# GpSimd issues its transfers by index in pairs and waits for each pair's landing

## Chip, core and metric

The kernel runs on one core of one Trainium2 chip. The core has five engines that run their own programs and meet at semaphores: TensorE (PE), VectorE (DVE), ScalarE (ACT), GpSimd (POOL) and SyncE (SP). The metric is the device time of one launch in microseconds, median of the timed runs.

## What is computed

A stack of residual layers over x of 32 x 256 tokens with 128 numbers each. The part that matters here is the feed-forward L0_ffn, which stands before and after an attention and sends each token to two of eight experts:

```python
def _L0_ffn_ref(x, gate_w, gate_b, w1, b1, w3, b3, w2, b2, sw1, sb1, sw3, sb3, sw2, sb2):
    xt = x.reshape(-1, D)
    logits = xt @ gate_w.T
    scores = jax.nn.softmax(logits.astype(jnp.float32), axis=-1)
    biased = scores + gate_b.astype(jnp.float32)
    idx = jax.lax.top_k(biased, TOP_K)[1]
    weights = (jnp.take_along_axis(scores, idx, axis=-1) * ROUTE_SCALE).astype(x.dtype)
    cw = jnp.sum(jax.nn.one_hot(idx, E, dtype=x.dtype) * weights[..., None], axis=1)
    h1 = jnp.einsum('td,efd->etf', xt, w1) + b1[:, None, :]
    h3 = jnp.einsum('td,efd->etf', xt, w3) + b3[:, None, :]
    a = swiglu(h1 * h3)
    y = jnp.einsum('etf,edf->etd', a, w2) + b2[:, None, :]
    routed = jnp.einsum('te,etd->td', cw, y)
    sh = swiglu((xt @ sw1.T + sb1) * (xt @ sw3.T + sb3))
    shared = sh @ sw2.T + sb2
    return (routed + shared).reshape(inp_shape)
...
x = x + 0.5 * _L0_ffn_ref(_layernorm(x, axis=-1), ...)
x = x + _L0_attn_ref(_layernorm(x, axis=-1), ...)
x = x + 0.5 * _L0_ffn_ref(_layernorm(x, axis=-1), ...)
x = x + 0.5 * _L1_ffn_ref(_layernorm(x, axis=-1), ...)
x = x + _L1_attn_ref(_layernorm(x, axis=-1), ...)
x = x + 0.5 * _L1_ffn_ref(_layernorm(x, axis=-1), ...)
```

## The kernel before

**Tiling.** The 8192 tokens are 16 chunks of 512; a chunk is 4 tiles of 128 tokens, one a partition. x stays in the on-chip memory for the whole run. The 16 chunks form three groups of 4, 6 and 6. The two passes of L0_ffn are l = 0 and l = 1; the attention lies at the start of the second pass.

**One pass for a group.** A "head" step normalises a chunk, makes the gate's logits and the shared expert's part, and leaves the rows in fp16 halves in `rows` (a view of `store`). The "route" steps on DVE choose two experts and compute for each token its place among its expert's rows, `r_slot`. POOL then *scatters*: for tile t and choice i one indirect DMA (L1914) writes 128 rows of 512 bytes from `rows` to the table `row_dram[g]` in HBM, at the places in `r_slot`. When all scatters of the group have landed, SP loads the table's rows back, transposed, into `u_xp` (L1979, `load_rows`, which waits for `scattered[g]`), PE, ACT and DVE run the experts on them in units of 512 rows, and ACT stores the results to the table `ys` in HBM. POOL *fetches*: for a chunk eight indirect DMAs (L1930), by choice and tile, each 128 rows of 512 bytes from `ys` to `y_in` at the places in `r_result`. There are two buffers `y_in`, for even and odd chunks. DVE waits for all eight (`fetched[c % 2]`), multiplies them by the weights and adds them to x (L1135, `weighed`). There are 128 x 2 = 256 scatters and 256 fetches.

**POOL's other work** are the small powers for the norms: `rstd_entry` (L1880), `rstd_head` (L1885), `gn_r_head` (L1895), `rstd_mid`, `rstd_front` and `rstd_last` (L1874, L1876). DVE or ACT wait for each of them.

**Order.** Each engine runs its steps in an order that is written out by hand, as a string of letters for each engine (`turns`); for POOL "s" is one scatter step (two DMAs), "f" one fetch, "a", "b" and "c" are the heads of three lanes. Two heads' work is interleaved with two lanes of units. `Waiting.wait_ge` leaves out a wait for a value that the engine has already waited for. Before the change POOL waits for no landing of its own DMAs: it goes on when a DMA's descriptors are made. A DMA adds 16 to its semaphore when it has landed.

Of the kernel before, what the change touches and what calls it, by code (L numbers as in the profile page):

```python
# [20 lines left out]
T = 4  # L21
# [119 lines left out]
def build(nc, dram, packed, x_in, out):  # L141
# [14 lines left out]
    with ExitStack() as ctx:  # L156
# [1711 lines left out]

        def pool_program(pool):
            on = Waiting(pool)  # L1870

            def root(s, which, c, a, b):
                on.wait_ge(*s.by_vector.at("mv", which, c))
# [32 lines left out]
            def scatter(l, g, t):  # L1906
                c = groups[g].first + t // T
                on.wait_ge(*route.by_vector.at("slot", l, c // 2))
                on.wait_ge(*heads[c % LANES].by_vector.at("rows", l, c))
                if l:  # L1910
                    for u in (groups[g].units - 2, groups[g].units - 1):
                        on.wait_ge(*unit_lanes[u % 2].by_tensor.at("h", l - 1, g, u, 0, 0))
                for i in range(2):
                    pool.indirect_dma_start(  # L1914
                        row_dram[g], bass.IndirectOffsetOnAxis(route.slot[g][:, i, t:t + 1].bitcast(U32), 0),
                        rows[:, groups[g].first * T + t, :, :].rearrange("p k d -> p (k d)"), None).then_inc(scattered[g], 16)

            def fetches(l, c, n):
                g, t0, i = group_of[c], (c - groups[group_of[c]].first) * T, c % 2
                k, t = divmod(n, T)  # L1920
                if n == 0:
                    for j in range(2):
                        last = load_index((l, g, groups[g].units - 1))
                        on.wait_ge(y_stored[(last + j) % 2], 16 * ((last + 1 + j) // 2))
                    on.wait_ge(*route.by_vector.at("result", l, g))
                    if l or c >= 2:
                        l2, c2 = divmod(l * chunks + c - 2, chunks)
                        reader = mids[c2 % 2] if l2 else heads[c2 % LANES]
                        on.wait_ge(*reader.by_vector.at("weighed", l2, c2, 1))
                pool.indirect_dma_start(  # L1930
                    fetch.y[i][:, t, k, :], None, y_dram[g],
                    bass.IndirectOffsetOnAxis(route.result[g][:, k, t0 + t:t0 + t + 1].bitcast(U32), 0)).then_inc(fetched[i], 16)
# [256 lines left out]
```

## Time and profile before

| | us |
|---|---|
| three timed runs: median (lowest to highest) | 1219.88 (1218.39 to 1219.9) |
| the profiled execution, first to last instruction | 1611.3 |
| of it busy: PE, DVE, ACT, POOL | 1208.2, 1037.9, 881.7, 645.2 |
| POOL in 256 scatters, in 256 fetches | 258.8, 262.2 |
| POOL waiting for its issue before scatters, before fetches | 70.8, 70.3 |

The profiled execution is a third longer than the timed ones. Its durations are read one by one, and its idle times with care: a timed run has less of them. A POOL row of a DMA is the time in which POOL makes its descriptors, not the time to its landing. "issue" is a gap that nothing visible released. Waits of an engine stand under the instruction that waited, with what released it.

### The profile page before, as it was taken

How to read it: one execution, taken by the hardware profiler on the slowest of the kernel's cores; microseconds unless marked ns; L12 is line 12 of the kernel's file. 1: busy time of each engine (PE TensorE's matmuls, PEld its weight loads, DVE VectorE, ACT ScalarE, POOL GpSimd, SP SyncE). 2: the span in 40 equal slices, each digit the busy share in tenths (PEclk: the TensorE clock that was granted, in tenths of full speed). 3: DMA queues.
4: the chain of work that ended last, by engine and by line, in shares of the span. 5: the costliest groups of instructions: out<-in, count | busy, mean ns of one | idle time of the engine just before them, and what ended most of it. 6: DMA issues, size and time to landing. Idle time of an engine off the chain costs nothing.

```text
span 1611.3 us, 37336 instructions
## 1 busy us (share of the span) xinstructions
PE 1208.2 (75%) x14084; PEld 950.7 (59%) x14113; DVE 1037.9 (64%) x3441; ACT 881.7 (55%) x1505; POOL 645.2 (40%) x679
## 2 busy tenths in 40 slices
PE   3745767567766778767666766799989897989997
PEld 2423545455555666555554645677877676768776
DVE  7954655455645656666664664677767757888774
ACT  3545556334544445645543653676677445766764
POOL 1364443344555455555545453431322323342100
PEclk9876878787887978988887887898898978999989
DMA  8012323223132322222132222311210101010001
GB/s 263 14 50 62 79 68 75 59 63 83 57 84 70 78 71 76 62 65 55 57 87 67 68 67 66 76 43 46 56 46 23 28 18 33 15 29 24 2 9 34
DMA packets 172875, 93.77 MB, mean 58 GB/s; under 512 B 98516, under 2 KB 163183, under 8 KB 172575
## 3 DMA queue, kind: packets, MB, share of 16 engines
q1 hardware_dynamic: 115886, 35.64, 9.0%
q0 software_dynamic: 16384, 33.59, 7.3%
q10 hardware_dynamic: 40432, 22.17, 4.9%
q8 instruction: 118, 1.93, 0.5%
q14 instruction: 55, 0.44, 0.1%
HBM read 25.78 MB, written 45.61 MB: 44 GB/s over the span
## 4 chain that ended last, share of the span: by engine, by line
PE 37%; DVE 22%; ACT 13%; another core or an unknown queue 13%; issue 12%; POOL 1%; DMA 1%; ACTq 0%; POOLq 0%; DVEq 0%; SPq 0%
PE bank L759 8%; PE bank L581 3%; PE bank L820 2%; PE bank L967 2%; PE bank L806 2%; PE bank L839 2%; DVE x L1135 2%; PE bank L775 2%; PE sums L984 1%; PE sums L901 1%; PE bank L532 1%; PE sums L904 1%; ACT heads_store L1674 1%; DVE heads_store L1189 1%
## 5 line engine op out<-in xcount | busy, mean ns | idle before, releaser
L1914 POOL DMA_INDIRECT rows<-store,r_slot x256 | 258.8, 1011 | 185.1 <-DVE r_slot L1396 114.1
L759 PE MATMUL bank<-u_xp,w_hi 128*128 128x128 f16 x2432 | 267.3, 237 | 83.7 <-issue 74.0
L1930 POOL DMA_INDIRECT y_in<-ys,r_result x256 | 262.2, 1024 | 120.6 <-issue 70.3
L759 PE MATMUL bank<-u_xp,w_lo 128*128 128x128 f16 x1216 | 245.7, 237 | 34.6 <-issue 34.4
L759 PEld LDWEIGHTS bank<-u_xp,w_hi 128*128 x2432 | 212.3, 108 | 100.0 <-issue 94.4
L759 PEld LDWEIGHTS bank<-u_xp,w_lo 128*128 x1216 | 130.3, 107 | 47.1 <-issue 47.1
L581 PE MATMUL bank<-heads_store,w_hi 128*128 128x512 f16 x256 | 92.6, 449 | 7.0 <-DVE r_lg L1164 4.2
L1874 POOL TENSOR_SCALAR ve_last<-mv_last 128x4 f32<-128x4 f32 x16 | 3.1, 195 | 215.0 <-DVE mv_last L1092 214.9
L1698 ACT ACTIVATE heads_store<-bank,sc 128x512 f32<-128x512 f32 x64 | 43.3, 682 | 75.0 <-PE bank L581 41.1
L1135 DVE SCALAR_TENSOR_TENSOR x<-y_in,r_weight,x 128x128 f32<-128x128 f32 x256 | 72.5, 346 | 1.1
L1189 DVE TENSOR_TENSOR heads_store<-bank,heads_store 128x512 f32<-128x512 f32 x64 | 43.7, 686 | 42.7 <-ACT heads_store L1698 33.9
L1885 POOL TENSOR_TENSOR rstd_head<-ve_head,half_neg 128x4 f32<-128x4 f32 x32 | 34.6, 1082 | 88.1 <-DVE ve_head L1097 86.8
L1481 DVE TENSOR_TENSOR u_gated_even<-bank,u_gated_even 128x512 f32<-128x512 f32 x38 | 26.0, 685 | 66.7 <-ACT u_gated_even L1769 34.6
L1665 ACT COPY heads_store<-bank 128x1024 f16<-128x1024 f16 x32 | 32.3, 1009 | 54.6 <-remote 32.3
L967 PE MATMUL bank<-store 32*64 32x64 f32 x2048 | 49.6, 239 | 15.6 <-issue 12.1
L1625 DVE TENSOR_TENSOR store<-store,bank 128x512 f32<-128x512 f32 x64 | 40.9, 681 | 25.0 <-PE bank L967 14.9
L581 PE MATMUL bank<-heads_store,w_lo 128*128 128x512 f16 x128 | 56.7, 443 | 0.0
L1895 POOL TENSOR_TENSOR gn_r_head<-gn_ve_head,half_neg 128x2 f32<-128x2 f32 x16 | 11.9, 742 | 109.7 <-DVE gn_ve_head L1334 109.7
L967 PEld LDWEIGHTS bank<-store 32*64 32x64 f32 x2048 | 41.8, 149 | 22.8 <-issue 17.9
L1769 ACT ACTIVATE u_linear_odd<-bank,sc 128x512 f32<-128x512 f32 x38 | 26.0, 683 | 50.1 <-PE bank L759 25.9
L1481 DVE TENSOR_TENSOR u_linear_odd<-bank,u_linear_odd 128x512 f32<-128x512 f32 x38 | 26.1, 687 | 40.3 <-remote 15.7
L1769 ACT ACTIVATE u_gated_odd<-bank,sc 128x512 f32<-128x512 f32 x38 | 26.0, 684 | 47.1 <-remote 37.3
(434 smaller groups left out, 3478.4 us busy)
## 6 DMA issues: line engine op xcount, KB each, us to landing
ys<-u_y_even ACTq DMA_DIRECT2D x38, 256.0 KB
ys<-u_y_odd ACTq DMA_DIRECT2D x38, 256.0 KB
u_xp<-rows SPq DMA_TRANSPOSE x304
x<-x_dram SPq DMA_DIRECT2D x16, 256.0 KB, 5.6
rows<-store,r_slot POOLq DMA_INDIRECT x256
y_in<-ys,r_result POOLq DMA_INDIRECT x256
out_dram<-x SPq DMA_DIRECT2D x16, 256.0 KB
rows<-blank SPq DMA_DIRECT2D x48, 64.0 KB
```

Source lines behind the costliest of these rows:

```text
L581: ins = pe.matmul(B[:], wp[:, part, E, which, :], s.xp[:, xp, :], start=(n == 0), stop=(n == 2))
L759: ins = pe.matmul(B[:, of_block[j]], of_expert(wp, e, F16, part, which), xp_rows[:, xp, of_block[j]], start=(n == 0 and j == 0), stop=(n = ...
L967: ins = pe.matmul(B[i][halves[u], col:col + HALF], kt[strip[i], tokens], qpt[slot][strip[i], tokens], start=True, stop=True)
L1135: ins = dve.scalar_tensor_tensor(xt, y[:, t, i, :], w[:, i, t0 + t:t0 + t + 1], xt, ALU.mult, ALU.add)
L1189: s.by_vector.mark(dve.tensor_tensor(h, ring[s.name, "h", l, c, part, 1][:], h, ALU.mult), "h", l, c, part)
L1481: s.by_vector.mark(dve.tensor_tensor(h[:], ring["units", "h", l, g, u, part, 1][:], h[:], ALU.mult), "h", *use, part)
L1625: mark(dve.tensor_tensor(s.att[g], s.att[g], ring[s.name, "att", c, g][:], ALU.mult), "att", c, g)
L1698: s.by_scalar.mark(act.activation(t, ring[s.name, "h", l, c, part, 0][:], ACT.Copy, scale=sc31[:]), "h", l, c, part)
L1769: s.by_scalar.mark(act.activation(t[:], ring["units", "h", l, g, u, part, 0][:], ACT.Copy, scale=sc31[:]), "h", *use, part)
L1885: s.by_pool.mark(pool.tensor_tensor(s.rstd[:], s.ve[:], half_neg[:], ALU.pow), "rstd", which, c)
L1914: pool.indirect_dma_start(row_dram[g], bass.IndirectOffsetOnAxis(route.slot[g][:, i, t:t + 1].bitcast(U32), 0), rows[:, groups[g].first * ...
L1930: pool.indirect_dma_start(fetch.y[i][:, t, k, :], None, y_dram[g], bass.IndirectOffsetOnAxis(route.result[g][:, k, t0 + t:t0 + t + 1].bitc ...
```

## The change

POOL keeps a list of its transfers by index that are under way, scatters and fetches in one list in the order of issue. `previous_landed` is called ahead of each. When the third enters, POOL waits until the second one's semaphore shows its landing, and drops the first two from the list. So ahead of every odd transfer from the third on (255 of 512) POOL waits for the transfer before it. In a pair of two scatters of a group, or two fetches into one buffer, the awaited count covers both; in 40 pairs the two have different semaphores, and the count is that of the second alone.

```diff
--- before.py
+++ after.py
@@ -1868,6 +1868,13 @@
 
         def pool_program(pool):
             on = Waiting(pool)
+            in_flight = []
+
+            def previous_landed(landing, value):
+                in_flight.append((landing, value))
+                if len(in_flight) == 3:
+                    on.wait_ge(*in_flight[1])
+                    del in_flight[0:2]
 
             def root(s, which, c, a, b):
                 on.wait_ge(*s.by_vector.at("mv", which, c))
@@ -1911,6 +1918,7 @@
                     for u in (groups[g].units - 2, groups[g].units - 1):
                         on.wait_ge(*unit_lanes[u % 2].by_tensor.at("h", l - 1, g, u, 0, 0))
                 for i in range(2):
+                    previous_landed(scattered[g], 16 * (2 * groups[g].tiles * l + 2 * t + i + 1))
                     pool.indirect_dma_start(
                         row_dram[g], bass.IndirectOffsetOnAxis(route.slot[g][:, i, t:t + 1].bitcast(U32), 0),
                         rows[:, groups[g].first * T + t, :, :].rearrange("p k d -> p (k d)"), None).then_inc(scattered[g], 16)
@@ -1927,6 +1935,7 @@
                         l2, c2 = divmod(l * chunks + c - 2, chunks)
                         reader = mids[c2 % 2] if l2 else heads[c2 % LANES]
                         on.wait_ge(*reader.by_vector.at("weighed", l2, c2, 1))
+                previous_landed(fetched[i], 16 * (2 * T * (l * (chunks // 2) + c // 2) + n + 1))
                 pool.indirect_dma_start(
                     fetch.y[i][:, t, k, :], None, y_dram[g],
                     bass.IndirectOffsetOnAxis(route.result[g][:, k, t0 + t:t0 + t + 1].bitcast(U32), 0)).then_inc(fetched[i], 16)
```

The instructions of all engines stay the same and in the same order. POOL, near the end of the second pass (names with 2 are the last group's, `ys0` and `result0` the first group's). Before the change:

```order
L1885 TENSOR_TENSOR rstd_head0<-ve_head0,half_neg 128x4 [waits head0_by_vector]
L1914 DMA rows2<-store,r_slot2 28672x256 x4
L1930 DMA y_in0<-ys0,r_result0 128x128
L1874 TENSOR_SCALAR ve_mid1<-mv_mid1 128x4 [waits mid1_by_vector]
L1876 TENSOR_TENSOR rstd_mid1<-ve_mid1,half_neg 128x4 [waits mid1_by_pool]
L1914 DMA rows2<-store,r_slot2 28672x256 [waits head1_by_vector]
L1914 DMA rows2<-store,r_slot2 28672x256 x7
L1914 DMA rows2<-store,r_slot2 28672x256 [waits head2_by_vector,route_by_vector]
L1914 DMA rows2<-store,r_slot2 28672x256 x7
L1914 DMA rows2<-store,r_slot2 28672x256 [waits head0_by_vector]
```

and with it:

```order
L1892 TENSOR_TENSOR rstd_head0<-ve_head0,half_neg 128x4 [waits head0_by_vector]
L1922 DMA rows2<-store,r_slot2 28672x256 [waits y_fetched0]
L1922 DMA rows2<-store,r_slot2 28672x256
L1922 DMA rows2<-store,r_slot2 28672x256 [waits scattered2]
L1922 DMA rows2<-store,r_slot2 28672x256
L1939 DMA y_in0<-ys0,r_result0 128x128 [waits scattered2]
L1881 TENSOR_SCALAR ve_mid1<-mv_mid1 128x4 [waits mid1_by_vector]
L1883 TENSOR_TENSOR rstd_mid1<-ve_mid1,half_neg 128x4 [waits mid1_by_pool]
L1922 DMA rows2<-store,r_slot2 28672x256 [waits head1_by_vector]
L1922 DMA rows2<-store,r_slot2 28672x256 [waits scattered2]
L1922 DMA rows2<-store,r_slot2 28672x256
L1922 DMA rows2<-store,r_slot2 28672x256 [waits scattered2]
```

Each second scatter or fetch now carries a wait on `scattered2` or `y_fetched0`, and the pairs don't follow tiles or kinds: a fetch can be the first of a pair whose second is a scatter. The root `rstd_mid1` stands behind such a wait.

POOL again, between the fetches of two groups. Before:

```order
L1885 TENSOR_TENSOR rstd_head1<-ve_head1,half_neg 128x4 [waits head1_by_vector]
L1914 DMA rows1<-store,r_slot1 28672x256 x4
L1930 DMA y_in0<-ys2,r_result2 128x128 x2
L1885 TENSOR_TENSOR rstd_head0<-ve_head0,half_neg 128x4 [waits head0_by_vector]
L1930 DMA y_in0<-ys2,r_result2 128x128
L1930 DMA y_in1<-ys2,r_result2 128x128 x8
L1930 DMA y_in0<-ys0,r_result0 128x128 [waits head2_by_vector,y_stored0,y_stored1]
L1930 DMA y_in0<-ys0,r_result0 128x128 x3
L1885 TENSOR_TENSOR rstd_head2<-ve_head2,half_neg 128x4 [waits head2_by_vector]
L1895 TENSOR_TENSOR gn_r_head1<-gn_ve_head1,half_neg 128x2 [waits head1_by_vector]
```

and with the change:

```order
L1892 TENSOR_TENSOR rstd_head0<-ve_head0,half_neg 128x4 [waits head0_by_vector]
L1939 DMA y_in0<-ys2,r_result2 128x128
L1939 DMA y_in1<-ys2,r_result2 128x128 [waits y_fetched0]
L1939 DMA y_in1<-ys2,r_result2 128x128
L1939 DMA y_in1<-ys2,r_result2 128x128 [waits y_fetched1]
L1939 DMA y_in1<-ys2,r_result2 128x128
L1939 DMA y_in1<-ys2,r_result2 128x128 [waits y_fetched1]
L1939 DMA y_in1<-ys2,r_result2 128x128
L1939 DMA y_in1<-ys2,r_result2 128x128 [waits y_fetched1]
L1939 DMA y_in1<-ys2,r_result2 128x128
L1939 DMA y_in0<-ys0,r_result0 128x128 [waits head2_by_vector,y_fetched1,y_stored0,y_stored1]
L1939 DMA y_in0<-ys0,r_result0 128x128
```

The eight fetches into `y_in1` are now four waits for a landing, and the first fetch of the next group waits for a landing beside what it waited for already.

## Rows read from the trace of the kernel before

**Rows 1.** The page: span, busy time, and forty slices of PE and POOL.
```profile
span 1611.3 us, 37336 instructions
PE 1208.2 (75%) x14084; PEld 950.7 (59%) x14113; DVE 1037.9 (64%) x3441; ACT 881.7 (55%) x1505; POOL 645.2 (40%) x679
...
PE   3745767567766778767666766799989897989997
POOL 1364443344555455555545453431322323342100
```

**Rows 2.** Busy time by stretch; columns in the first line.
```profile
core 0: us, PE busy (x) PEld busy (x) DVE busy (x) ACT busy (x) POOL busy (x), PEclk, DMA share, GB/s
0.00:400.00 400.00, 250.20 (x2122) 176.00 (x2122) 243.42 (x843) 194.07 (x317) 164.37 (x171) 0.80 0.29 81
400.00:1000.00 600.00, 421.06 (x3866) 337.28 (x3868) 351.56 (x1214) 297.79 (x489) 311.88 (x312) 0.84 0.26 69
1000.00:1480.00 480.00, 420.80 (x6068) 342.67 (x6086) 352.99 (x1124) 306.09 (x546) 159.36 (x180) 0.88 0.14 37
1480.00:1611.30 131.30, 116.10 (x2035) 94.79 (x2040) 89.90 (x264) 83.75 (x156) 9.62 (x16) 0.95 0.06 18
```

**Rows 3.** Waits of POOL, 400 to 1000 us: in total, times, longest.
```profile
POOL gn_r_head L1895 <- DVE gn_ve_head L1334: 92.3, 13, 14.0
POOL rstd_head L1885 <- DVE ve_head L1097: 78.1, 17, 10.5
POOL rows L1914 <- issue: 40.5, 139, 0.3
POOL y_in L1930 <- issue: 34.0, 118, 0.3
```

**Rows 4.** The scatters (L1914) by stretch: POOL busy, count, clock, DMA share, GB/s.
```profile
400.00:1000.00 600.00, 148.65 (x146) 0.84 0.26 69
```

**Rows 5.** The fetches (L1930), 400 to 1000 us, in the same columns.
```profile
400.00:1000.00 600.00, 119.84 (x120) 0.84 0.26 69
```

**Rows 6.** Timeline of POOL, 801 to 805 us: start, duration, line, [idle before].
```profile
801.44 0.98 POOL L1914 DMA_INDIRECT rows<-store,r_slot  x1 [0.31 <-issue]
802.72 0.98 POOL L1914 DMA_INDIRECT rows<-store,r_slot  x1 [0.30 <-issue]
804.01 1.03 POOL L1914 DMA_INDIRECT rows<-store,r_slot  x1 [0.30 <-issue]
```

**Rows 7.** Timeline of SP: transposes that wait for the scatters of one group.
```profile
806.42 2.50 SPq L1979 DMA_TRANSPOSE u_xp<-rows  x2
```

**Rows 8.** Timeline of SP: the same wait for the last group's scatters.
```profile
997.30 2.51 SPq L1979 DMA_TRANSPOSE u_xp<-rows  x2
```

**Rows 9.** Timeline of POOL: first and last of 16 scatters in a row.
```profile
956.69 0.97 POOL L1914 DMA_INDIRECT rows<-store,r_slot  x1 [10.28 <-DVE r_slot L1396]
...
976.77 0.97 POOL L1914 DMA_INDIRECT rows<-store,r_slot  x1 [0.31 <-issue]
```

**Rows 10.** Timeline of POOL: a root, then fetches; the 496.67 one fills its buffer.
```profile
492.32 1.03 POOL L1885 TENSOR_TENSOR rstd_head<-ve_head,half_neg 128x4 f32<-128x4 f32 x1 [10.49 <-DVE ve_head L1097]
...
496.67 1.12 POOL L1930 DMA_INDIRECT y_in<-ys,r_result  x1 [0.30 <-issue]
```

**Rows 11.** Timeline of DVE: the products with that buffer.
```profile
498.68 0.68 DVE L1189 TENSOR_TENSOR heads_store<-bank,heads_store 128x512 f32<-128x512 f32 x1
499.38 2.32 DVE L1135 SCALAR_TENSOR_TENSOR x<-y_in,r_weight,x 128x128 f32<-128x128 f32 x8
```

**Rows 12.** The page: DMA queues, then the chain that ended last.
```profile
q1 hardware_dynamic: 115886, 35.64, 9.0%
q0 software_dynamic: 16384, 33.59, 7.3%
...
PE 37%; DVE 22%; ACT 13%; another core or an unknown queue 13%; issue 12%; POOL 1%; DMA 1%; ACTq 0%; POOLq 0%; DVEq 0%; SPq 0%
```

**Rows 13.** The longest wait on any engine, 1000 to 1611 us.
```profile
POOL ve_last L1874 <- DVE mv_last L1092: 214.9, 15, 29.5
```

## The prediction, made before the changed kernel ran

> **What bounds the kernel now.** Start with the page [rows 1]: no engine is full. In the slices PE stands at 6 to 8 tenths for the first 25 of the 40 slices and at 8 to 9 after them, and POOL at 3 to 5 tenths for the first 26 and 1 to 4 later. The profiled execution took 1611.3 us, the timed ones 1219.88 at the median: the profiled one is 391.4 us longer, and its idle time is therefore no measure of the idle time that the timed runs have. This is the point on which the whole prediction turns, so it is worked out first.
>
> Read busy time by stretch [rows 2]. From 1000 us to the end (611.3 us) DVE is busy 353.0 + 89.9 = 442.9 us. DVE's work is there in the timed run too, so this stretch can give back at most 611.3 - 442.9 = 168.4 of the 391.4 us. At least 391.4 - 168.4 = 223 us must come out of the first 1000 us, which in a timed run last at most 777. Spread evenly, the stretch from 400 to 1000 us (second pass of the feed-forward: fetches of the first pass, attention, scatters of the second) lasts at most 600 x 0.777 = 466 us. By the plain ratio 1219.88 / 1611.3 = 0.757 it lasts 454. I take 454.
>
> Now POOL in that stretch. It is busy 311.9 us [rows 2], and before 257 of its instructions stands a gap of about 0.3 us that nothing releases, 40.5 + 34.0 = 74.5 us [rows 3]. Together POOL is occupied 386.4 us: 64% of the profiled 600, but 85% of the 454. Where the profile shows 214 us in which POOL waits for others (170.4 of it for DVE's ve_head and gn_ve_head [rows 3]), the timed run has about 68. That POOL has 1% of the chain that ended last [rows 12] says only that it is in time today.
>
> **What the change adds.** No transfer is added, removed or moved. Before each odd transfer by index (the third, fifth, and so on; 255 of 512) POOL now waits until the one before it has landed. POOL runs its program in order, so everything behind the waiting transfer waits too: its own pair, the roots rstd_head, gn_r_head, rstd_mid and rstd_front for which DVE's next steps wait, and the last scatter of a group, for which SP's transposes wait.
>
> Price of one wait. Today transfers follow each other every 1.28 us: 801.44 to 802.72, and 804.01 [rows 6]. How long one needs to land the profile doesn't list, so it is bounded. The scatter that starts at 804.01 is the last of its group, and SP's transposes, which wait for it, start at 806.42 [rows 6, 7]: 2.41 us with SP's own waking in it. So a pair's successor starts 2.41 - 1.28 = 1.13 us later than today. For a fetch: the one that starts at 496.67 completes a buffer, and the products that wait for it start at 499.38 [rows 10, 11], 2.71 us, or 2.71 - 1.27 = 1.44 later; DVE was busy until 499.36, so this is an upper end only. The lower end: a transfer can't land before its 0.97 us on POOL are over [rows 9], which alone would add nothing. I take 1.0 us, near the scatter's 1.13, as that row is the same kind of wait. The Trainium skill (DMA: Bandwidth & Descriptors, Anatomy of one DMA) puts a DMA issued by GpSimd at about 2.0 us plus bytes / 436e3; for 64 KB this is 2.15 us, so by the page a wait would add 0.87, an estimate, and the sum below would be some 14 us smaller. The rows' 2.41 and 2.71 agree with it, each being a little above.
>
> How many waits cost it. In the stretch 400 to 1000 us there are 146 scatters and 120 fetches [rows 4, 5], so 133 waits. A wait costs its full price only where the transfer follows the former at once; where a root or an idle time lies between, it has landed. Along POOL's timeline 110 of the 133 follow within 2.2 us. So POOL's load becomes 386.4 + 110 x 1.0 = 496 us, against 454 (or at most 466) us in which it has to be done: 42 us too much (30 with 466), and by the price of 1.13 it is 57. A further cause in the other direction: POOL's order is fixed and its inputs come from a chain (fetch, product, root, attention, root, scatter), so some of its idle time can't be filled.
>
> The other stretches. Up to 400 us POOL is busy 164.4 us; with about 39 us of gaps and 53 such waits it is 256 of 303 us (400 x 0.757): covered, and a few us late at the ends of groups. After 1000 us it is 169 us busy, has 99 gaps and some 35 such waits, about 232 of 463 (611.3 x 0.757): covered, since POOL's longest wait there is for DVE's mv_last, 214.9 us [rows 13]. I put 3 us on both.
>
> Sum: 42 + 3 = 45 us, 1219.88 + 45 = **1265 us**, 3.7% slower. In the profiled execution, where POOL keeps 104 us of idle time in the stretch (600 - 496), the same change must cost far less: I expect its span to grow by 5 to 40 us.
>
> **Rivals.**
>
> *The cover holds.* POOL catches up in each of its idle times, as it would in the profiled execution. For this: fetches run ahead (buffers for two chunks), and in the last group, 16 scatters in a row from 956.69 to 976.77 [rows 9] would end 8 us later, while SP starts their transposes only at 997.30 [rows 8]. Against: the 85% load above. What is left then is the end of a group: six of them, each with two to four waits right before the end [rows 6, 7], so 2 to 4 us each if PE has nothing else, 16 us; and single roots behind a waiting transfer, as the one at 492.32 would be [rows 10], a few us. It gives 1220 to 1240 us.
>
> *The delays feed each other.* Each chunk passes POOL four times (fetch, two roots of the norms, one of the attention, scatter), and three chunks are in work at a time. If each of 16 chunks in 3 lanes loses 1 us at three roots and 4 us at its fetches, this is 5.3 x 7 = 37 us on top of the load: 1300 us and up, to about 1340.
>
> *Faster.* Fetches and scatters in flight share the 16 DMA engines with the transposes: POOL's queue holds 7.3% of the engines' time, the queue of the transposes 9.0%, and 13% of the chain (206 us) ended at something the profile can't name, most likely landings [rows 12]. With at most two of POOL's transfers in flight these could land sooner. The Trainium skill (DMA: Bandwidth & Descriptors, Queues, rings and completion order) says that an engine goes round its queues a packet at a time, which would have that effect. But only 1.28 us lies between two issues, so today about two are in flight anyway, and the engines are busy 26% in the stretch [rows 4]. A tenth of the 206 us saved and a load that fits gives about 1205 us. It decides if a landing became shorter by more than 20 us in all before POOL is full.
>
> *The waits do nothing.* If transfers landed before the next is ready, or the waits were dropped as known already, all stays at 1220. The two transposes at 806.42 speak against a landing within 1.28 us, and the order shows the 255 waits. In pairs of a scatter and a fetch only the second one's count is waited for, which changes no time.
>
> **How the numbers follow.** POOL becomes the bound of the second pass, 1240 to 1295 us: 0.55. Cover holds, 1220 to 1240: 0.23, of which 0.05 within 0.2%. Feeding each other, 1295 to 1340: 0.12. Faster: 0.05. Nothing: 0.05. About 0.2% (2.4 us) is what a measurement of this kernel can tell from no change. So faster 0.05, same 0.10, slower 0.85. The range leaves out the faster and the unchanged cases and the upper part of the feeding one: 1224 to 1312 us.
>
> **What would show it.** In the profile after: transfers in the timeline in pairs, 1.28 us apart within a pair and 2.2 to 2.4 from a pair's second to the next first (price). "rows <- issue" and "y_in <- issue" [rows 3] replaced by waits of about 1.3 us for a landing, some 110 of them between 400 and 1000 us (count). POOL's waits for ve_head and gn_ve_head, 170.4 us today, falling by 60 us or more (that POOL's idle time is eaten). DVE and ACT waiting more in that stretch and hardly more after it (place). The prediction is wrong if POOL's spacing of 1.28 us is the profiler's and not the kernel's, if a landing takes under 2 us, or if the timed run's time lies elsewhere than the even spread says, so that the second pass has more room than 454 us.

## The result

The changed kernel takes **1507.08 us** at the median, the kernel before 1219.86: ratio 1.2345, 95% interval 1.2302 to 1.2389, 23% slower. The forecast was 1265 us in a range of 1224 to 1312: the direction was right, the size was six times too small (45 us forecast, 287 measured). One of the changed kernel's four executions took 2027.1 us, at a granted clock of 1.0 where the others have 0.88; it is counted as a slow one, the ratio leaves it out, and its cause is not known.

The page on which the prediction rests [rows 1] shows an execution of 1611.3 us, not one of the timed 1219.88. The changed kernel's profiled execution took 1508.76 us, like its timed ones, and the kernel before was profiled a second time and took 1217.07 us, so recording by itself costs nothing. This second profile is what the changed kernel is compared with. The time of the kernel before was measured again beside every run below: about 1222 us (1222.45 or 1222.71) unless the text says otherwise.

The page of the changed kernel, the lines that answer to [rows 1, 12] and POOL's two groups (line, engine, operation, count | busy, mean ns | idle before, what ended most of it):

```profile
span 1506.9 us, 37356 instructions
PE 1132.1 (75%) x14084; PEld 920.4 (61%) x14113; DVE 1034.3 (69%) x3441; ACT 878.5 (58%) x1505; POOL 644.8 (43%) x679
...
PE   3766865377676776666677676699899898989997
POOL 1355554455554555555555564442523344441000
...
DMA 36%; POOL 18%; DVE 17%; PE 13%; issue 11%; ACT 5%; POOLq 0%; SPq 0%; ACTq 0%; DVEq 0%
DMA rows<-store,r_slot 20%; DMA y_in<-ys,r_result 15%; POOL rows L1922 8%; POOL y_in L1939 6%; PE bank L820 1%; POOL rstd_head L1892 1%; PE bank L759 1%; PE bank L839 1%; PE bank L967 1%; DVE store L1625 1%; DVE x L1135 1%; PE sums L984 1%; PE bank L806 1%; PE bank L883 1%; DVE mid_store L1103 1%
...
L1922 POOL DMA_INDIRECT rows<-store,r_slot x256 | 259.6, 1014 | 281.3 <-DMA rows<-store,r_slot 192.3
L1939 POOL DMA_INDIRECT y_in<-ys,r_result x256 | 262.6, 1026 | 264.5 <-DMA y_in<-ys,r_result 189.0
```

POOL had 1% of the chain [rows 12]; now POOL and the landings of its transfers are 54% of it, and the two groups of transfers are idle 281.3 + 264.5 us before them, mostly for landings. POOL's busy time is what it was (645.2 and 644.8 us).

The kernel before, second profile, in the same lines:

```profile
span 1215.1 us, 37336 instructions
PE 1058.3 (87%) x14084; PEld 855.3 (70%) x14113; DVE 1030.7 (85%) x3441; ACT 875.8 (72%) x1505; POOL 653.7 (54%) x679
...
PE   2877889898899988889888899989989999899997
POOL 1177776777777787877887643241333464420010
...
DVE 38%; PE 24%; ACT 16%; POOL 8%; issue 7%; SPq 3%; DMA 2%; ACTq 0%; POOLq 0%; DVEq 0%
```

Busy times are those of [rows 1] to within 1.5% (DVE 1030.7 for 1037.9, POOL 653.7 for 645.2), except PE's, which gets a higher clock. But the idle time is gone, and not evenly: POOL stands at 7 to 8 tenths (once at 6) from the third slice to the 22nd. The end of that is the last scatter, at 676.7 us (976.77 in [rows 9]). Both kernels in the stretch from 80 us to the last scatter follow: busy times (in the columns of [rows 2]), and under them POOL's waits (total us, times, longest). The kernel before:

```profile
80.00:677.00 597.00, 520.16 (x5665) 424.88 (x5664) 521.34 (x1794) 448.38 (x744) 459.27 (x456) 0.97 0.41 104
```

```profile
POOL rows L1914 <- issue: 69.7, 237, 0.3
POOL y_in L1930 <- issue: 42.1, 146, 0.3
POOL rows L1914 <- DVE r_slot L1396: 10.4, 7, 3.2
POOL rstd_head L1885 <- DVE ve_head L1097: 6.1, 5, 2.4
POOL y_in L1930 <- DMA ys<-u_y_odd: 3.6, 2, 2.1
POOL gn_r_head L1895 <- DVE gn_ve_head L1334: 3.5, 5, 1.4
```

and the changed kernel:

```profile
80.00:946.00 866.00, 585.62 (x5719) 485.61 (x5718) 523.52 (x1791) 452.96 (x747) 451.54 (x455) 0.84 0.28 72
```

```profile
POOL rows L1922 <- DMA rows<-store,r_slot: 189.4, 104, 3.6
POOL y_in L1939 <- DMA y_in<-ys,r_result: 107.1, 58, 3.0
POOL y_in L1939 <- DMA rows<-store,r_slot: 26.0, 16, 2.5
POOL rows L1922 <- DMA y_in<-ys,r_result: 21.5, 11, 2.9
POOL rows L1922 <- issue: 41.1, 130, 2.2
POOL y_in L1939 <- issue: 21.2, 74, 0.3
```

In the kernel before POOL is busy 459.3 of 597 us, its gaps of 0.3 us take 111.8, and it waits for others for 24.5 us (the rows shown and a few of 0.3): it is full to 96%. In the changed kernel POOL is busy 451.5 us, waits 344.0 us for landings (189 times), has 62.3 us of gaps and 6.5 us of other waits. So +344.0 - 49.5 - 18.0 - 7.8 = +269 us, and the stretch is 866 - 597 = 269 us longer. That the terms add up proves nothing: busy times, gaps and waits of any engine fill its stretch. What tells is which term grew and which vanished: waits for landings came in, and POOL waits for other engines for only 6.5 of 866 us, so it is POOL that sets the pace. The other 22 us lie behind the last scatter (560.6 us for 538.4; 553.8 us, so 15, in a second profile of the changed kernel, e12). DVE's busy time in the stretch is the same (523.5 and 521.3).

### The profile page after: what moved, and what is told of

It is laid out like the page before. It is cut to its first block, busy times and chain, and to the rows that moved or that the text cites. A ratio compares the mean times of both kernels' runs of the same rounds, so it can differ in the third digit from the quotient of the medians.

```text
span 1506.9 us, 37356 instructions
## 1 busy us (share of the span) xinstructions
PE 1132.1 (75%) x14084; PEld 920.4 (61%) x14113; DVE 1034.3 (69%) x3441; ACT 878.5 (58%) x1505; POOL 644.8 (43%) x679
## 4 chain that ended last, share of the span: by engine, by line
DMA 36%; POOL 18%; DVE 17%; PE 13%; issue 11%; ACT 5%; POOLq 0%; SPq 0%; ACTq 0%; DVEq 0%
DMA rows<-store,r_slot 20%; DMA y_in<-ys,r_result 15%; POOL rows L1922 8%; POOL y_in L1939 6%; PE bank L820 1%; POOL rstd_head L1892 1%; PE bank L759 1%; PE bank L839 1%; PE bank L967 1%; DVE store L1625 1%; DVE x L1135 1%; PE sums L984 1%; PE bank L806 1%; PE bank L883 1%; DVE mid_store L1103 1%
## 5 line engine op out<-in xcount | busy, mean ns | idle before, releaser
L1922 POOL DMA_INDIRECT rows<-store,r_slot x256 | 259.6, 1014 | 281.3 <-DMA rows<-store,r_slot 192.3
L1939 POOL DMA_INDIRECT y_in<-ys,r_result x256 | 262.6, 1026 | 264.5 <-DMA y_in<-ys,r_result 189.0
L759 PE MATMUL bank<-u_xp,w_hi 128*128 128x128 f16 x2432 | 246.2, 233 | 90.8 <-DMA u_xp<-rows 47.7
L759 PEld LDWEIGHTS bank<-u_xp,w_hi 128*128 x2432 | 206.2, 106 | 104.0 <-issue 99.0
L759 PE MATMUL bank<-u_xp,w_lo 128*128 128x128 f16 x1216 | 235.7, 233 | 1.0 <-issue 1.0
L759 PEld LDWEIGHTS bank<-u_xp,w_lo 128*128 x1216 | 128.5, 106 | 1.2 <-issue 1.2
L532 PE MATMUL bank<-w_packed,heads_store 128*128 128x128 f32 x128 | 24.9, 327 | 53.8 <-DVE heads_store L1103 51.4
L839 PE MATMUL bank<-a_w,heads_store 128*128 128x408 f32 x128 | 51.8, 546 | 17.3 <-ACT heads_store L1662 17.0
L1103 DVE TENSOR_SCALAR heads_store<-x,mv_head,rstd_head 128x128 f32<-128x128 f32 x64 | 18.9, 356 | 62.5 <-POOL rstd_head L1892 62.5
L1728 ACT ACTIVATE heads_store<-heads_store,gn_bi_head,gn_sc_head 128x256 f32<-128x256 f32 x32 | 17.4, 592 | 74.6 <-DVE gn_bi_head L1342 74.6
L1662 ACT COPY heads_store<-bank 128x512 f32<-128x512 f32 x32 | 18.7, 583 | 71.5 <-PE bank L532 37.4
L772 PE MATMUL bank<-by_expert,r_member 128*128 128x128 bf16 x304 | 33.1, 238 | 35.8 <-DVE u_linear_odd L1474 14.3
L1769 ACT ACTIVATE u_gated_even<-bank,sc 128x512 f32<-128x512 f32 x38 | 25.9, 682 | 55.1 <-PE bank L759 53.9
L532 PEld LDWEIGHTS bank<-w_packed,heads_store 128*128 128x128 f32 x128 | 18.0, 171 | 59.5 <-issue 39.0
L1625 DVE TENSOR_TENSOR store<-store,bank 128x512 f32<-128x512 f32 x64 | 40.8, 679 | 16.3 <-ACT store L1851 10.4
L775 PE MATMUL bank<-w_packed,u_linear_odd 128*128 x304 | 51.7, 324 | 0.0
```

Source lines behind the costliest of these rows:

```text
L532: ins = pe.transpose(M[:, by_t[t]], s.xn[:, t, :], ident[:])
L759: ins = pe.matmul(B[:, of_block[j]], of_expert(wp, e, F16, part, which), xp_rows[:, xp, of_block[j]], start=(n == 0 and j == 0), stop=(n = ...
L772: pe.matmul(Y[:, of_block[j]], members(use)[:, j:j + 1].broadcast_to([P, BLOCK]), by_expert[:, 0, :], start=(j == 0), stop=False, skip_gro ...
L775: ins = pe.matmul(Y[:, of_block[j]], s.linear[:, of_block[j]], of_expert(w2_bytes, held[use][j], F32), start=False, stop=(j == PER_UNIT - ...
L839: s.by_tensor.mark(pe.matmul(B[:, 0:3 * D + 3 * NH1], s.xt[:, by_t[t]], a1_w[:], start=True, stop=True), "qkv", c, t)
L1103: ins = dve.tensor_scalar(out[:, t, :], xc(c)[:, t, :], s.mv[:, t, 0:1], s.rstd[:, t:t + 1], ALU.subtract, ALU.mult)
```

## The experiments

Three theories are set against each other. Theory A: until the last scatter POOL's time is the bound, and whatever occupies POOL there is paid one for one. Theory B: it is the landing that costs, since few transfers are in flight and rows and results come late. Theory C: before the change something else is the bound, and POOL has room.

The table sorts the profiled runs by POOL's account, in us, between 80 us and the last scatter. "landing" is the sum of POOL's waits that a landing of its own transfers ended, "gaps" of those that nothing visible ended, "other" of all others. The medians stand beside 1222 us for the kernel before (1219.86 for the changed kernel itself). The runs beside which the kernel before took 1616 us (e9, e10, e11) stand apart, further down.

| run | median, us | last scatter at | POOL busy | landing (times) | gaps | other | after the last scatter |
|---|---|---|---|---|---|---|---|
| kernel before (e1) | 1221.81 | 676.7 | 459.3 | 0 | 111.8 | 24.5 | 538.4 |
| roots off POOL (e7) | 1220.43 | 676.3 | 403.2 | 0 | 113.8 | 78.9 | 551.3 |
| waits only after the last scatter (e14) | 1236.10 | 678.1 | 456.4 | 0 | 111.9 | 28.1 | 554.3 |
| one wait in eight (e2) | 1280.43 | 728.2 | 453.6 | 74.6 (42) | 103.3 | 16.6 | 547.4 |
| two in flight, rolling (e4) | 1296.91 | 746.5 | 453.5 | 156.4 (228) | 47.9 | 6.9 | 544.3 |
| fetches only (e6) | 1327.12 | 769.8 | 451.3 | 120.0 (58) | 95.2 | 22.1 | 556.3 |
| scatters only (e5) | 1332.20 | 785.4 | 453.0 | 147.0 (89) | 87.8 | 16.5 | 539.1 |
| short computing (e13) | 1344.84 | 802.2 | 621.1 | 0 | 90.9 | 4.0 | 541.2 |
| pairs, roots off POOL (e8) | 1494.02 | 928.5 | 399.6 | 372.7 (191) | 65.1 | 11.7 | 560.9 |
| changed kernel | 1507.08 | 946.3 | 451.5 | 344.0 (189) | 62.3 | 6.5 | 560.6 |
| long computing (e3) | 1549.30 | 983.3 | 802.9 | 0 | 89.9 | 4.4 | 560.6 |
| a wait for each (e15) | 1825.15 | 1232.4 | 451.9 | 682.0 (386) | 11.7 | 4.9 | 590.8 |

**The kernel before, profiled again (e1).**

> The kernel before, unchanged, for a second profile of it. The page of before shows a span of 1611.3 us while its timed runs take 1219.88, and the changed kernel's profiled run (1508.8) agrees with its timed ones. Theory A (profiling itself costs nothing, the page of before shows an execution of another kind): this profile has a span near 1218 us, with DVE again about 1035 us busy and POOL about 645, so that from the start to the last scatter it takes about 740 us instead of 977. Theory B (recording stretches this kernel, and hides in the changed one behind POOL's waits): the span is again near 1610 us.

Measured: 1221.81 us, ratio 1.0015 (0.9983 to 1.0047), span 1215.1 us. Its rows stand above. The first expectation held, but with a last scatter at 677 us and not at 740: the even shrinking by 0.757 was wrong.

**Computing in the place of waiting (e3).** No wait for a landing; POOL computes a power that nobody reads.

```diff
...
-                    on.wait_ge(*in_flight[1])
+                    if spent_count:
+                        on.wait_ge(spent_sem, len(spent_count))
+                    spent_count.append(1)
+                    pool.tensor_tensor(spent[:], ages[:], ages[:], ALU.pow).then_inc(spent_sem, 1)
...
```

> In the place of each of the 255 waits POOL computes a power of 128 x 8 numbers that nobody reads (by the rows of 128 x 2 and 128 x 4 about 1.6 us), and waits for no landing. Theory A (POOL's time is the bound): like the changed kernel, 1450 to 1540 us. Theory B (the landing itself matters: too few transfers in flight, so rows and results come late): as before or a little more, 1220 to 1290 us.

Measured: 1549.3 us, ratio 1.2675 (1.2624 to 1.2726). The computing (count, then duration min/median/max in ns) and the stretch:

```profile
L1882 POOL TENSOR_TENSOR spent<-ages x255: 1622/1671/2512, 62.2 to 1397.5; 128x8 f32<-128x8 f32 x128
```

```profile
80.00:983.00 903.00, 589.42 (x5717) 486.19 (x5716) 525.16 (x1794) 453.04 (x747) 802.93 (x655) 0.82 0.26 69
```

No landing is waited for, and the kernel is even slower than the changed one: so the price can be paid without a single wait for a landing, by POOL's occupied time alone. This run doesn't separate the number in flight, however. From the second transfer of a pair to the next one there are 2.86 us here, longer than the 2.62 to 2.80 at which the changed kernel goes on after a landing, so here too seldom more than two are under way:

```profile
598.26 0.98 POOL L1945 DMA_INDIRECT y_in<-ys,r_result  x1 [0.30 <-issue]
599.26 1.67 POOL L1882 TENSOR_TENSOR spent<-ages 128x8 f32<-128x8 f32 x1
601.12 1.01 POOL L1945 DMA_INDIRECT y_in<-ys,r_result  x1 [0.19 <-issue]
```

The next run and the rolling limit (e4) separate it.

**The short computing (e10, e13).** The same edit with 128 x 2 numbers.

> The short power (128 x 2, 0.72 us) in the place of each of the 255 waits, again, as its first job ran on the chip where the kernel before takes 1616 us. Account of POOL's time, on a chip where the kernel before takes 1222: 202 x 0.72 = 145 us before the last scatter, less 18 us of idle time: 1340 to 1375 us. If POOL has more room than that: 1290 to 1330 us.

Measured (e13): 1344.84 us, ratio 1.1047 (1.0962 to 1.1131), within the expected 1340 to 1375. POOL's busy time in the stretch grew by 162 us, gaps and other waits fell by 41, the last scatter moved by 125. Here the distance is 1.96 us (594.98 to 596.94), too short for the transfer before to have landed (the shortest landing of a scatter in e15 is 2.22 us after its start), and the added time is paid all the same:

```profile
594.98 1.00 POOL L1928 DMA_INDIRECT rows<-store,r_slot  x1 [0.30 <-issue]
596.00 0.73 POOL L1882 TENSOR_TENSOR spent<-ages 128x2 f32<-128x2 f32 x1
596.94 1.04 POOL L1928 DMA_INDIRECT rows<-store,r_slot  x1 [0.20 <-issue]
```

The first run of this kernel, on a chip of which more is said below, took 1398.16 us.

**A wait for each transfer (e9, e15).**

```diff
-                if len(in_flight) == 3:
-                    on.wait_ge(*in_flight[1])
-                    del in_flight[0:2]
+                if len(in_flight) == 2:
+                    on.wait_ge(*in_flight[0])
+                    del in_flight[0]
```

> POOL waits for the landing before every transfer (511 waits), so only one is ever in flight. Account of POOL's time: in the changed kernel 189 waits for a landing of 1.82 us stand between 80 us and the last scatter at 946 us, in the place of gaps of 0.3 us. With 405 transfers in that stretch and some 60 of them behind a root, about 345 waits of 1.5 us are added to the 677 us of the kernel before, less its 18 us of idle time: last scatter at about 1175 us, and the rest, with 107 waits among POOL's idle times, 40 to 60 us over its 538: 1740 to 1800 us in all. If it was the wait itself and not its length (each wait worth 287 / 255 = 1.13 us): 511 x 1.13 = 575, about 1800 us, so only the place of the last scatter and the sum of the landing waits (account: 500 to 540 us) tell these apart.

> A wait for the landing before each transfer (511 waits), again for the same reason; on the third chip it took 1824 us with 669.5 us of landing waits before its last scatter at 1221 us. Beside 1222: the same account, 1740 to 1830 us, last scatter 1175 to 1225 us.

Measured: 1824.35 us (e9) and 1825.15 us (e15), ratio of the latter 1.4921 (1.4856 to 1.4986). The median is at the upper end, since the 386 waits are 682 us and not 500 to 540: each is 1.77 us long on average, and takes the place of a gap of 0.3. In POOL's account +682.0 - 100.1 - 19.6 - 7.4 = +555 us; the last scatter moved by 556, to 1232.4 us, a little behind the 1175 to 1225 expected for e15.

**Once in eight (e2).**

```diff
-                if len(in_flight) == 3:
-                    on.wait_ge(*in_flight[1])
-                    del in_flight[0:2]
+                if len(in_flight) == 9:
+                    on.wait_ge(*in_flight[7])
+                    del in_flight[0:8]
```

> POOL waits for a landing once in eight transfers (63 waits) and not once in two (255). Theory A (POOL's time is the bound: in the changed kernel 232 waits for a landing of 1.85 us each stand where a gap of 0.3 us stood, 1.55 us apiece or 360 us, and POOL's own reserve took up 360 - 287 = 73 us): 63 x 1.55 = 98 us, less the reserve, 1220 to 1265 us. Theory B (each wait for a landing costs the kernel its share, whatever POOL's load): 63/255 of 287 us is 71 us, about 1290 us.

Measured: 1280.43 us, ratio 1.0476 (1.0434 to 1.0519), between the two expectations. Theory A's own number (1220 to 1265) was too low since it put POOL's reserve at 73 us. The table shows 24.5 us of other waits before and 16.6 here: only 8 us of them could be used.

**Two in flight, rolling (e4).** Before transfer n POOL waits for n - 2. Each semaphore is split in two by the parity of the transfer, so that the counts are exact.

```diff
-                if len(in_flight) == 3:
-                    on.wait_ge(*in_flight[1])
-                    del in_flight[0:2]
+                if len(in_flight) == 3:
+                    on.wait_ge(*in_flight[0])
+                    del in_flight[0]
...
-                    previous_landed(scattered[g], 16 * (2 * groups[g].tiles * l + 2 * t + i + 1))
+                    previous_landed(scattered[g][i], 16 * (groups[g].tiles * l + t + 1))
```

> Never more than two transfers in flight, as in the changed kernel, but rolling: before transfer n POOL waits for transfer n - 2 (each kind's semaphore is split in two so that the counts are exact; the engines that wait for all wait for both halves). A scatter lands and wakes POOL about 2.5 us after its start, a fetch about 2.85, and n would start 2.55 us after n - 2 in any case. Theory A (POOL's time is the bound): next to nothing for scatters, up to 0.15 us for each fetch, 1220 to 1270 us. Theory B (a limit of two in flight is what costs): about 1500 us.

Measured: 1296.91 us, ratio 1.0615 (1.0551 to 1.0679). The same limit of two in flight as in the changed kernel costs 74 us and not 287: with e3 and e13 this is what lets theory B fall. It is more than theory A expected (1220 to 1270): its 228 landing waits are 0.69 us on average, 0.4 more than a gap.

**Scatters only, fetches only (e5, e6).** One of the two calls of `previous_landed` is left out.

> Only the scatters are issued in pairs with a wait for the landing (127 waits); fetches go out as before. Theory A (POOL's time up to the last scatter is the bound): all these waits lie in the stretch where POOL is full, 127 x 1.55 us = 197 us at most, less where fetches or roots stand between two pairs and cover the landing: 1350 to 1420 us. Theory B (what costs is that results come back late to DVE, so the fetches matter): little, 1220 to 1270 us.

> Only the fetches are issued in pairs (127 waits); scatters go out as before. Theory A: of the 256 fetches about 150 are issued before the last scatter, so about 75 waits of 1.6 us stand in the full stretch, 120 us at most, and the other 50 lie where POOL has idle time and cost next to nothing: 1290 to 1345 us. Theory B (results come back late): most of the 287 us, 1400 us and more.

Measured: 1332.2 us (ratio 1.0907, 1.0853 to 1.0961) and 1327.12 us (1.0841, 1.077 to 1.0913). Scatters came out under the expectation of 1350 to 1420: only 89 of 127 waits are left to be waited for, most likely since other transfers and roots stand between two pairs. Fetches are within it, and far from theory B's 1400. The two don't add up to 287 but to 214; their landing waits add up to 267 of the 344 us. The likely reason, not tested by itself, is that in the changed kernel a pair of one kind no longer has the other kind's transfers, free of waits, behind it to hide its landing. With fetches alone the part behind the last scatter grows to 556.3 us, with scatters alone it stays at 539.1.

**Only behind the last scatter (e11, e14).**

```diff
-                    previous_landed(scattered[g], 16 * (2 * groups[g].tiles * l + 2 * t + i + 1))
...
-                previous_landed(fetched[i], 16 * (2 * T * (l * (chunks // 2) + c // 2) + n + 1))
+                if (l, c, n) >= (1, 2, 5):
+                    previous_landed(fetched[i], 16 * (2 * T * (l * (chunks // 2) + c // 2) + n + 1))
```

> Pairs and waits only for the 107 fetches after POOL's last scatter (53 waits), again for the same reason. Account of POOL's time, beside 1222: last scatter where it is in the kernel before (677 us), the rest 538 to 556 us, 1222 to 1242 us in all. If a late landing costs wherever it stands: about 1300 us.

Measured (e14): 1236.1 us, ratio 1.0132 (1.0091 to 1.0172). POOL's longest waits from the last scatter to the end:

```profile
POOL ve_last L1881 <- DVE mv_last L1092: 150.1, 13, 29.8
POOL y_in L1939 <- DMA y_in<-ys,r_result: 94.8, 46, 4.6
POOL ve_mid L1881 <- DVE mv_mid L1092: 56.6, 11, 10.1
```

46 waits of 94.8 us cost 14 us here: POOL has idle time, and its three waits for DVE's moments (mv_last, mv_mid, mv_front) give up 56 us in all (307.3 to 251.7). The waits are not free, 0.3 us each for a mean length of 2.06 us.

**Roots off POOL (e7, e8).** DVE makes a reciprocal in the place of POOL's power, so the heads' norms divide by the variance and the square root is left out; tokens may go to other experts by it, in the same number of transfers. The main lines of the edit:

```diff
...
+                    if s in heads:
+                        on.wait_ge(*at("ve", *point))
+                        mark(dve.reciprocal(s.rstd[:], ve), "rstd", *point)
...
-                j = k - 11 if l else k
-                if l and j == 0:
-                    head_root(s, ("ffn0", l), c)
...
+                return
...
```

> The kernel before, with POOL's 48 roots for the heads (32 rstd_head of 1.04 us, 16 gn_r_head of 0.74 us) taken off POOL; DVE makes a reciprocal of the same size in their place, so the norms of the heads divide by the variance and not by its root, and nothing else is left out. Theory A (POOL is already the bound before the change, up to its last scatter): POOL has 48 x 1.0 = 48 us less, DVE some 10 us more, and the time falls by 10 to 45 us, to 1175 to 1212 us. Theory C (before the change DVE is the bound, and POOL only becomes it by the waits): 1220 to 1235 us.

> The changed kernel, with the same 48 roots taken off POOL (the same reciprocals on DVE in their place, the norms of the heads computed otherwise). Theories A and C alike (POOL is the bound with the waits): a root between two pairs covers a part of a landing, so between a half and all of the 48 us comes back, 1455 to 1485 us. Theory B (only landings matter): 1500 us or more, as DVE has more to do.

Measured: 1220.43 us (ratio to the kernel before 0.9985, 0.9953 to 1.0018) and 1494.02 us (13 us less than the changed kernel's 1507; 1.2216, 1.2158 to 1.2275). Theory A missed both (1175 to 1212 and 1455 to 1485). The profiled execution of e7 was its slowest (1229.37 us), which may be why its part behind the last scatter is as long as 551.3 us. The kernel before with the roots off POOL:

```profile
80.00:676.00 596.00, 518.12 (x5648) 422.09 (x5646) 525.92 (x1837) 447.00 (x743) 403.17 (x407) 0.98 0.42 104
```

```profile
POOL rows L1913 <- DVE r_slot L1403: 63.0, 11, 11.6
```

POOL has 56 us less to do, waits for others 54 us more (78.9 us, of which 63.0 for DVE's r_slot, 10.4 before), and the last scatter comes at the same 676 us. So theory A in the form "POOL alone is the bound before the change" is wrong. POOL is full to 96% and can't take on more, yet the kernel has nothing to win by freeing it. DVE, busy 526 of 596 us here, and PE, 518, are nearly full too; that the three hold each other up in their fixed orders fits this, but no run frees DVE or PE to show it. Theory C's number (1220 to 1235) held here, but not its claim that POOL has room: in e13 nearly all that was added was paid. In e8 a root gone is in good part a longer wait for the same landing: busy -51.9, landing +28.7 us.

**The changed kernel again (e12).**

> The changed kernel once more, beside the kernel before on the same chip. In the last job the kernel before took 1616 us in every run and had a granted clock of 0.85, where it had taken 1222 at 0.97 on two other chips; its first profile (1611.3 us) was of this kind. If this chip is like the first two: 1507 us beside 1222. If it is like the third: if POOL's waits bound the changed kernel, what disturbs the kernel before is hidden behind them, 1510 to 1560 beside 1616; if the disturbance adds to them, near 2000, as one run of the changed kernel did (2027).

Measured: 1508.02 us beside 1222.45, ratio 1.2347 (1.2268 to 1.2425); POOL's landing waits are those of the first profile (344.0 us, 190 times), its waits for others 11.8 us.

**On the third chip (e9, e10, e11).** There the kernel before took 1616.18 us in the median of seven runs (1609.93 to 1622.13), at a granted clock of 0.85. Beside it: waits for each 1824.35 us, short computing 1398.16, waits only behind the last scatter 1567.06. The kernel with the most waits takes there what it takes elsewhere (1824 and 1825), and the one with short computing is 218 us *faster* than the kernel before.

> Like the run in which POOL computes in the place of each wait, with 128 x 2 numbers and not 128 x 8: by the row of gn_r_head 0.72 us and not 1.67. Account of POOL's time: some 202 of the 255 stand before the last scatter, 202 x 0.72 = 145 us, less 18 us of POOL's idle time there: last scatter near 805 us, 1340 to 1375 us in all. If POOL has more room than that (taking 48 us of roots off it gained nothing), 1290 to 1330 us.

> Pairs and waits only for the 107 fetches that POOL issues after its last scatter (53 waits), where it waits over 300 us for DVE's moments. Account of POOL's time: the part after the last scatter grows as it did where the fetches had waits (538 to 556 us) or less, 1222 to 1242 us. If a late landing costs wherever it stands: 53 x 1.5 = 80 us, about 1300 us.

Both times lie above what POOL's account gave (1340 to 1375 and 1222 to 1242), but neither answers the question asked of it, as the kernel before is itself disturbed there; e13 and e14 ask again beside 1222 us.

## Why the prediction was wrong

**What held.** The direction; the place (the stretch up to the last scatter, 269 of 292 us by the two spans); the mechanism (POOL becomes the bound there); that what is behind the last scatter is nearly covered. Of the signs named for it, pairs and waits for landings came, but larger: 2.62 to 2.80 us from a pair's second to the next for 2.2 to 2.4, waits of 1.82 us for 1.3. The sign "waits for ve_head and gn_ve_head fall by 60 us" can't be judged: in the 1215.1 us execution they are 9.6 us up to the last scatter, not 170.4. POOL in the changed kernel (start, duration, [idle before]):

```profile
566.00 1.01 POOL L1939 DMA_INDIRECT y_in<-ys,r_result  x1 [0.19 <-issue]
568.84 0.96 POOL L1939 DMA_INDIRECT y_in<-ys,r_result  x1 [1.82 <-DMA y_in<-ys,r_result]
570.11 0.96 POOL L1939 DMA_INDIRECT y_in<-ys,r_result  x1 [0.30 <-issue]
572.91 0.95 POOL L1939 DMA_INDIRECT y_in<-ys,r_result  x1 [1.84 <-DMA y_in<-ys,r_result]
574.17 1.01 POOL L1922 DMA_INDIRECT rows<-store,r_slot  x1 [0.30 <-issue]
576.79 0.99 POOL L1922 DMA_INDIRECT rows<-store,r_slot  x1 [1.61 <-DMA rows<-store,r_slot]
```

**Step 1, the room, failed most.** The prediction took the stretch from 400 to 1000 us as 454 us long in a timed run and POOL's load as 386.4 us, 85%. POOL's work between those two points (from its first root after 400 us to its first after 1000 us) takes 405 us in the second profile (from 278.7 to 684.1 us), and POOL needs 386 of them. The room was 19 us and not 68. The bound of 466 us holds, but it too rests on an even spread of the missing time inside the first 1000 us, for which there was no evidence, and so does the choice of 454. The missing time lay where the engines wait for each other most: the stretch up to the last scatter shrank by 0.69, the one behind it by 0.85 (634.5 to 538.4 us). In the first 400 us it was the same: 203 us of load and 53 of waits were set against 303 us, while that work took 279, and nearly all of POOL's idle time in it lies before 80 us, where the change has little to wait for (from 80 to 278.7 us POOL waits for others for 13 us).

**Step 2, the price, was a third too low.** 1.0 us was taken. The timeline above shows 2.80 us from the start of a pair's second fetch to the next (570.11 to 572.91) and 2.62 for a scatter (574.17 to 576.79), against 1.28 before the change: 1.5 and 1.3 us, and the mean over the 189 waits is 344.0 / 189 = 1.82 us of idle time for a gap of 0.3, 1.5 us. With one transfer in flight (e15) the landing itself can be read, from the increments of the semaphores that the trace records: a scatter's last one comes 2.29 us after its start at the median (2.53 on average), a fetch's 2.62 (2.76), and POOL's next transfer starts 0.26 us later. So a part of the price is POOL's own answer to the landing, a part are landings slower than the median. The scatter's row [rows 7] gave 1.13, by one landing to which SP and not POOL answered; the fetch's 1.44, discarded as an upper end, was nearly right. The Trainium skill (DMA: Bandwidth & Descriptors, Anatomy of one DMA) gives about 2.0 us plus bytes / 436e3 for such a DMA, an estimate of 2.15 us for 64 KB. The 2.29 us of the scatter are near it, the 2.62 of the fetch 0.5 above, and neither holds POOL's 0.26.

**Step 3, the count, was low.** 53 + 110 = 163 full waits were expected up to the last scatter; 189 are seen from 80 us on. The 110 were counted in the timeline of the 1611.3 us execution, where idle time before a transfer would have covered the landing; a full POOL starts its next transfer at once.

With the three corrected: 189 x 1.52 = 287 us, less the 18 us of other waits that POOL gave up, is the stretch's 269 us. This is a check of the form and not a second proof, since the terms are read from the changed kernel's own trace (and 0.3 us a gap is rounded: by the rows 49.5 us of gaps fell away, and 7.8 us of busy time). The 3 us for the rest should have been 15 to 22. So the sum's form was right, and its terms were not: the room stood at 68 + 100 us (454 - 386, 303 - 203) where 18 were to be had, and 163 x 1.0 stood where 189 x 1.52 was due.

**The forecast of the profile** (5 to 40 us more than 1611.3) can't be judged, since that execution was of another kind than the timed ones. That profile was said to be no measure of idle time, and the range was still built as if it nearly were: its upper end should have been the case of a POOL without room, 163 x 1.44 = 235 us and more.

**The rivals.** "The cover holds" was wrong up to the last scatter; behind it the cover did hold, all but 14 us (e14). "The delays feed each other" isn't needed: a delay that came back to POOL through the other engines would stand in its waits for them, and these fell from 24.5 to 6.5 us. "Faster" has no support: e4 has the same two in flight and is slower. Its 206 us at something the profile can't name belong to the 1611.3 us execution alone: the chain of the second profile has no such entry (and a tenth of 206 off 1220 is 1199 us, not 1205). The slices were read too evenly as well: PE stands at 3 to 8 tenths in the first 25, POOL at 1 to 6 in the first 26, and at 0 to 4 later; nothing in the sum hangs on it.

## What to carry over

Where an engine issues transfers one after another, a wait for a landing costs that engine the landing's time less one issue (here 1.5 us), and it is paid in full as soon as the engine has no idle time of its own; ask that of the stretch in which the wait stands, not of the whole span. If recorded and timed executions differ by more than a per cent or two, don't scale the idle time: the least room that the busy times allow belongs in the range. A limit on transfers in flight that rolls (wait for the one before the last) cost a quarter of the same limit in pairs here. And an engine that can't take on more isn't by that the one to relieve: 56 us less on POOL gained nothing before the change.

## What the runs showed of the hardware

- A transfer by index of 64 KB with nothing else of POOL's in flight (e15) lands 2.29 us (scatter to HBM) and 2.62 us (fetch from HBM) after its start at the median, and POOL's next one starts 0.26 us after that. The wait before it doesn't get much shorter than in pairs: 1.77 us of idle time on average, 1.82 in pairs.
- POOL alone needs 1.28 us from one such transfer to the next, about 1.0 busy and 0.3 of gap, about half of the time to a landing.
- The granted clock of TensorE, a mean over its two levels, was 0.97 in the kernel before up to the last scatter, with PE busy 520.2 of 597 us, and 0.84 in the changed kernel, with PE busy 585.6 of 866 us on the same matrix products. As POOL waits for others for 6.5 us there, little of this reached the time up to the last scatter. Behind it PE is busy 499.4 us for 491.2, and how much of the 22 us that makes isn't shown.
- One kernel can have two steady times. Beside e9 to e11 the kernel before took 1616 us in seven runs, beside all others about 1222. Whether the chip makes the difference isn't shown, since only these runs are known to be from that chip. The page of [rows 1] is of the long kind: DVE, ACT and POOL are busy as long as elsewhere (1037.9, 881.7, 645.2), but POOL waits for others for 330.5 us up to the last scatter, where it is 24.5 us in the second profile. The kernel with short computing on POOL was 14% faster there than the kernel before, and the one with a wait for each transfer took 1824 us there and 1825 elsewhere. What disturbs the long kind wasn't found. In the first profile the longest new gaps without a visible cause, 74 us, stand before PE's products of the units (L759). And the traces of the long kind (before, e10, e11) hold some 7300 to 7800 records of a landing's increments, those of all other runs 14400 to 15600: whether the records are missing by the same cause stays open.
